# A bias table's load moved to the front of the DMA queue, one PSUM clear and two routing steps moved beside the first maxima

## The chip, the cores and the metric

The kernel runs on one core of a Trainium2 chip. The metric is the device time of one execution in microseconds (us), over several executions; a profile of one execution gives the time of each instruction on the engines: TensorE (PE, its weight loads PEld), VectorE (DVE), ScalarE (ACT), GpSimd (POOL), SyncE (SP), and of the DMA engines that SyncE's queue feeds.

## What is computed

Two residual layers over x of 16 sequences of 256 tokens with 128 features. Each layer adds attention times silu of a mixture of experts. The change lies in the first layer alone, at the start of its attention, whose reference is (cut):

```python
    def _L0_attn_ref(x, Wq, bq, Wk, bk, Wv, bv, Wo, bo, rel_bias):
        N_HEADS = 16
        ...
        Q, K, V = (proj(Wq, bq), proj(Wk, bk), proj(Wv, bv))
        scores = jnp.einsum('bhqd,bhkd->bhqk', Q, K) / math.sqrt(D_K)
        scores = scores + _rel_bias_matrix(rel_bias, S)[None]
        attn = jax.nn.softmax(scores, axis=-1)
        out = jnp.einsum('bhqk,bhkd->bhqd', attn, V)
        ...
    def _L0_ffn_ref(x, W1, b1, W2, b2, gate_W, shared_W, shared_b, gamma, beta):
        ...
        probs = jax.nn.softmax(flat @ gate_W, axis=-1)
        topk_w, topk_idx = jax.lax.top_k(probs, TOP_K)
```

`_rel_bias_matrix` gives each head a table of 256 x 256 that depends on the distance of two tokens alone. The routing needs, for each token, its eight gate logits less their maximum, their exponentials, and the two largest.

## The kernel before

All engines run hand-written programs, ordered by semaphores alone; nothing is scheduled by a compiler. The work is in stages, and `b` counts the 16 sequences.

**Setup.** SyncE queues, on one queue, x, the weights, and two small DRAM strips made from the relative bias (`extb_dram` in bf16, `ext_dram` in fp32). From them two tables are loaded, 128 rows x 16 heads x 384: `biasA` (bf16, 1536 KB) for the maxima, `biasT` (fp32, 3072 KB) for the scores proper. `biasA` is loaded at once. `biasT` is loaded only after the next stage.

**Projection** (`pre_pe`, `pre_act`, `pre_dve`), 16 turns. PE multiplies (L680 for queries and keys into banks 6 and 7, L687 for values, gate logits and the shared expert). ACT copies queries and keys out (L1059, L1060), then rounds them to bf16, the "hi" piece (L1066); DVE takes values and logits (L1355, L1356), and splits off two more pieces (L1345, L1347, L1349). SyncE stores the three pieces to `stk_dram` in three DMAs per turn, 768 KB (L377), and loads the stacks of the first two sequences among them (L388, L389). The pieces have a ring of three, so L1066 of turn b waits until the stores of turn b - 3 have landed. `keep_shared` (L1070) copies the shared expert's part, one turn later than L1066 of the same turn.

**First maxima** (sequence 0), eight pairs of heads t. PE computes scores with bias in wide[0] and wide[1] in turn (`max_scores`: L719 bias, L725 scores), DVE reduces them (`reduce_maxima`, L1541). PE's first one waits for the semaphore `init` at 3, and for all of L1070. After `max_scores` of t = 5 PE transposes the first four pairs' maxima (L738), ACT copies them out (L1113, `copy_maxima`), SyncE places them in the stacks by DMA (L395, `place_maxima`, which also waits for all stores of pieces). Only then can PE make the first exact scores (`exp_scores`, L750).

**Attention**, sequence by sequence. In each turn t of sequence b PE makes the scores of b (L750) and the maxima's scores of b + 1 (L719, L725). Every other pair's scores are biased by DVE (`add_bias`, L1550), the others are copied by ACT (`take_scores`, L1129) and biased by POOL (L599); both read `biasT`. ACT takes the exponential (L1136). The steps of the first routing stand between DVE's turns of sequences 0 to 3 (L1388 to L1507).

**Between** projection and maxima stand three small things: `route_shift(0)` (L1381, L1382: maximum of the logits, and the difference), its exponential on ACT (`route_act`, L1094), and the clear of bank 6 (L1532), which adds the last count of `init`. Bank 6 is the target of queries and keys of the even turns, and later that of the attention's outputs.

Of the kernel before, what the change touches and what calls it, by code (L numbers as in the profile page):

```python
# [5 lines left out]
NB, S, D = 16, 256, 128  # L6
P = 128
T = NB * S // P
H0, DK = 16, 8
MAXREL = 128  # L10
NREL = 2 * MAXREL + 1
E0, E1, HID = 8, 4, 512
# [35 lines left out]
EXT = 2 * S - 1  # L48
# [12 lines left out]
BW = S + P  # L61
# [67 lines left out]
def build(nc, x, wpack, vectors, shb, relb, wcat0, wcat1, out):  # L129
# [10 lines left out]
    with ctx:  # L140
# [197 lines left out]
        def _(sp):  # L338
# [4 lines left out]
            for dst, src in ((packed[:, 0:3 * D], wpack[:, 0:3 * D]),  # L343
# [11 lines left out]
            sp.dma_start(biasA[:, :, :], bass.AP(tensor=extb_dram.tensor, offset=0, ap=[[1, P], [EXT, H0], [1, BW]])  # L355
                         ).then_inc(s_ba, 16)

            emptied = [0, 0]
# [43 lines left out]
            for b in range(NB // 2, NB):  # L402
# [4 lines left out]
                if first < 4:  # L407
                    load_stacks(first // 2, first // 2, first % 2)
            sp.dma_start(biasT[:, :, :], bass.AP(tensor=ext_dram.tensor, offset=0, ap=[[1, P], [EXT, H0], [1, BW]])
                         ).then_inc(s_bt, 16)  # L410
            for u in range(NRING):
# [621 lines left out]
        def _(act):  # L1033
# [14 lines left out]
            def pre_act():  # L1048
# [7 lines left out]
                def projected(b, u, turn):  # L1056
# [4 lines left out]
                    if b >= NRING:  # L1061
                        act.wait_ge(m[f"stored{b % NRING}"], b // NRING * STORES * 16)
                    act.wait_ge(m["qkf"], b + 3)
                    if b == 2:
                        act.wait_ge(s_extd, 32)
# [6 lines left out]

                staged([(transposed, 1), (projected, 2), (keep_shared, 3)])

# [21 lines left out]
            pre_act()  # L1096
            route_act(0, E0)

# [70 lines left out]
            fetch_values(0, 0)  # L1169
            copy_maxima(0, 0)  # L1170
            attend_act(0, 0, back=0)
            attend_act(1, 1, back=1)
# [105 lines left out]
        def _(dve):  # L1278
# [56 lines left out]
            def pre_dve(l, ne):  # L1335
# [15 lines left out]
                def logits(b, u, turn):  # L1351
                    dve.wait_ge(m["gs"], b + 3)
                    dst = some(lg, b * 2, 2)[:, :, 0:ne]
                    vg = wide[1 + u][:, :].rearrange("p (j c) -> p j c", j=2)
                    V.tensor_copy(dst, vg[:, :, D:D + E0]).then_inc(m["lg"], 1)  # L1355
                    V.tensor_copy(some(vall, b * 2, 2), vg[:, :, 0:D]).then_inc(m["v"], 1)  # L1356

                staged([(logits, 3), (split, 3)])
# [170 lines left out]
            dve.wait_ge(s_c, 11)  # L1529
            route_shift(0)  # L1530
            dve.wait_ge(pre[0]["qkf"], NB + 2)
            V.memset(bank[6][:, :], 0.0).then_inc(A0["init"], 1)  # L1532

# [67 lines left out]
            for t in range(NPAIR):  # L1601
                reduce_maxima(0, t)
            dve.wait_ge(s_bt, 16)
            attend_dve(0, back=0, part=0)
# [306 lines left out]
```

## Time and profile before

| | us |
|---|---|
| median of 3 runs | 900.63 |
| lowest, highest | 898.08, 901.89 |
| profiled execution, its own time | 896.93 |
| its span in the trace | 894.6 |
| PE busy | 732.0 (82%) |
| DVE busy | 570.2 (64%) |
| ACT busy | 494.3 (55%) |
| POOL busy | 450.1 (50%) |

The trace's times count from the start of the span; 2.3 us lie around it. PE is the busiest engine over the whole, but the change acts between 14 us and 90 us, and there other waits end last: they are read from the rows below. A timeline row tells when a group of instructions began, how long it lasted, and in square brackets how long its engine had been idle and what ended the idle time.

### The profile page before, as it was taken

What the parts mean: (1) busy time and instruction counts of PE and PEld (TensorE: products, weight loads), DVE (VectorE), ACT (ScalarE), POOL (GpSimd) and SP (SyncE); (2) the same over time, 40 slices, a digit from 0 to 9 for tenths busy, and PEclk for the clock granted to TensorE, in tenths of its full rate; (3) what the DMA queues carried; (4) which work ended last, traced back from release to release, by engine and by line L of the source; (5) the groups of instructions that cost most, each with busy time, mean ns of one, the idle gap of its engine ahead of it and who ended that gap; (6) DMA issues with size and microseconds to landing.
All of it is one profiled execution on the core that took longest, in us unless ns stands there. A gap on an engine that the chain in (4) does not pass through costs nothing.

```text
span 894.6 us, 17583 instructions
## 1 busy us (share of the span) xinstructions
PE 732.0 (82%) x5530; PEld 501.5 (56%) x5530; DVE 570.2 (64%) x1284; ACT 494.3 (55%) x949; POOL 450.1 (50%) x394
## 2 busy tenths in 40 slices
PE   0966597879999999988799998899947775999940
PEld 0741132233343334336799988789847664999940
DVE  7867989878888888842243357845547881344445
ACT  0752475558887888774355546579631352555521
POOL 7901454458888988851355544410006671555540
PEclk9997788789999999968999999999977796999985
DMA  7697440112322232124777896550001115787837
GB/s 212 228 284 265 155 156 19 49 57 70 99 77 77 79 94 84 57 79 125 232 233 225 235 300 203 176 159 1 2 0 46 46 55 150 230 230 230 231 115 186
DMA packets 112239, 124.08 MB, mean 139 GB/s; under 512 B 10544, under 2 KB 93152, under 8 KB 112192
## 3 DMA queue, kind: packets, MB, share of 16 engines
q1 hardware_dynamic: 104064, 106.71, 40.2%
q0 software_dynamic: 8128, 16.78, 5.3%
q8 instruction: 25, 0.41, 0.2%
q14 instruction: 22, 0.18, 0.1%
HBM read 82.50 MB, written 40.81 MB: 138 GB/s over the span
## 4 chain that ended last, share of the span: by engine, by line
PE 58%; DVE 19%; DMA 6%; issue 6%; ACT 5%; SPq 4%; POOL 1%; ACTq 0%; DVEq 0%; POOLq 0%
PE wide L855 15%; PE wide L844 14%; PE wide L765 6%; PE wide L719 4%; PE wide L750 4%; PE wide L777 3%; ACT work L1129 2%; PE wide L725 2%; DVE work L1550 2%; DMA work<-xg_dram 2%; DVE work L1541 2%; PE wide L929 2%; ACT work L1136 2%; PE wide L938 1%; DMA biasT<-ext_dram 1%
## 5 line engine op out<-in xcount | busy, mean ns | idle before, releaser
L635 POOL DMA_INDIRECT yg_dram<-work x138 | 134.3, 973 | 171.3 <-DVE work L1648 148.8
L1192 ACT ACTIVATE work<-wide,work 128x256 f32<-128x256 f32 x324 | 131.9, 472 | 112.4 <-PE wide L844 111.3
L1541 DVE TENSOR_REDUCE work<-wide 128x4 bf16<-128x1024 f32 x128 | 156.5, 1226 | 38.8 <-PE wide L725 37.0
L855 PE MATMUL wide<-work 128*128 128x128 f32 x1296 | 158.8, 276 | 0.0
L855 PEld LDWEIGHTS wide<-work 128*128 128x128 f32 x1296 | 153.2, 193 | 0.6
L844 PE MATMUL wide<-xT,work 128*128 128x256 f32 x552 | 134.9, 388 | 9.7 <-issue 6.2
L844 PEld LDWEIGHTS wide<-xT,work 128*128 128x128 f32 x552 | 101.7, 194 | 23.9 <-issue 8.1
L599 POOL TENSOR_TENSOR work<-work,biasT 128x1024 f32<-128x1024 f32 x32 | 75.8, 2368 | 75.6 <-ACT work L1129 75.0
L599 POOL TENSOR_TENSOR yy<-yy,biasT 128x1024 f32<-128x1024 f32 x32 | 75.7, 2366 | 42.6 <-ACT yy L1129 42.5
L719 PE MATMUL wide<-biasA,turnb 128*128 128x512 bf16 x256 | 83.8, 412 | 5.8 <-DVE wide L1532 5.0
L1136 ACT ACTIVATE yy<-yy 128x1024 f32<-128x1024 f32 x64 | 67.5, 1057 | 38.0 <-DVE yy L1550 38.0
L1620 DVE COPY xT<-wide 128x256 f32<-128x256 f32 x69 | 29.2, 423 | 92.8 <-PE wide L866 81.3
L750 PE MATMUL wide<-work 49*128 49x256 bf16 x512 | 54.5, 295 | 32.6 <-DVE yy L1550 18.0
L1136 ACT ACTIVATE work<-work 128x1024 f32<-128x1024 f32 x64 | 67.3, 1052 | 16.0 <-DVE work L1550 16.0
L591 POOL DMA_INDIRECT xg_dram<-bufB,sloti x64 | 62.8, 981 | 13.5 <-issue 12.3
L750 PEld LDWEIGHTS wide<-work 49*128 49x128 bf16 x512 | 15.1, 96 | 81.0 <-issue 26.2
L1645 DVE TENSOR_TENSOR work<-wide,work 128x256 f32<-128x256 f32 x69 | 29.2, 423 | 45.5 <-PE wide L855 45.4
L591 POOL DMA_INDIRECT xg_dram<-bufC,sloti x52 | 50.2, 965 | 15.8 <-issue 13.7
L725 PE MATMUL wide<-work 48*128 48x256 bf16 x512 | 53.2, 289 | 0.0
L725 PEld LDWEIGHTS wide<-work 48*128 48x128 bf16 x512 | 14.9, 96 | 60.4 <-issue 60.4
L587 POOL TENSOR_SCALAR bufC<-tokf 128x32 f32<-128x32 f32 x2 | 0.7, 325 | 88.6 <-DVE widx L1507 86.6
L1129 ACT ACTIVATE yy<-wide 128x1024 f32<-128x1024 f32 x32 | 32.7, 1021 | 18.8 <-PE wide L750 18.8
(273 smaller groups left out, 1273.1 us busy)
## 6 DMA issues: line engine op xcount, KB each, us to landing
work<-in_wcat SPq DMA_DIRECT2D x73, 578.0 KB
work<-stk_dram SPq DMA_DIRECT2D x128, 96.0 KB, 2.5
xg_dram<-empty SPq DMA_DIRECT2D x35, 260.0 KB, 2.5
work<-xg_dram SPq DMA_DIRECT2D x69, 130.0 KB
yy<-yg_dram SPq DMA_DIRECT2D x14, 512.0 KB, 6.9
stk_dram<-yy SPq DMA_DIRECT2D x16, 384.0 KB, 3.0
stk_dram<-yy SPq DMA_DIRECT2D x16, 256.0 KB, 3.1
biasT<-ext_dram SPq DMA_DIRECT2D x1, 3072.0 KB, 12.4
```

The source lines that it names most:

```text
L591: g.indirect_dma_start(out=xg_dram[l], out_offset=bass.IndirectOffsetOnAxis(ap=sloti[k][:, t:t + 1].bitcast(u32), axis=0), in_=xn_sb[l][:, ...
L599: g.tensor_tensor(sc, sc, bass.AP(tensor=bt.tensor, offset=bt.offset + S - 1, ap=[list(bt.ap)[0], [BW, 2], [P, 2], [-1, S]]), ALU.add).the ...
L635: g.indirect_dma_start(out=yg_dram[l], out_offset=bass.IndirectOffsetOnAxis(ap=yid[v][:, s_:s_ + 1].bitcast(u32), axis=0), in_=yb[u][:, s_ ...
L719: mm(PA[t % 2][:, e * 2 * S:(e + 1) * 2 * S], turnb[:, :], bass.AP(tensor=b_.tensor, offset=b_.offset, ap=[list(b_.ap)[0], [P, 2], [1, S]] ...
L725: last = mm(PA[t % 2][:, (2 * e + c) * S:(2 * e + c + 1) * S], qst[u][pair_rows(e, TROWS), t, qt * P:(qt + 1) * P], kst[u][pair_rows(e, TR ...
L750: last = mm(PB[:, (2 * e + k) * S:(2 * e + k + 1) * S], kst[u][pair_rows(e), t, k * P:(k + 1) * P], qst[u][pair_rows(e), t, :], start=True ...
L765: last = mm(PO[32 * i:32 * i + DK + 1, 0:S], vaug[u][:, k, 4 * gr + i, :], sc[:, at:at + S], start=(k == 0), stop=(k == 1))
L844: last = mm(HP[u][c // 2][:, (c % 2) * TS:(c % 2 + 1) * TS], wb[v][:, c * P:(c + 1) * P], rows, start=True, stop=True)
L855: last = mm(YP[u][:, s_ * D:(s_ + 1) * D], hb[u][:, c, s_ * P:(s_ + 1) * P], wb[v][:, HID + c * D:HID + (c + 1) * D], start=(c == 0), stop ...
L1136: A(scores[t], scores[t], ACT.Exp).then_inc(a["E"], 1)
L1192: A(hb[u][:, c, :], bank[2 + 2 * u + c // 2][:, (c % 2) * TS:(c % 2 + 1) * TS], ACT.Gelu, bias=wb[v][:, bc:bc + 1]).then_inc(m["gelu"], 1)
L1541: V.tensor_reduce(nmax[:, :, 2 * t:2 * t + 2].rearrange("p c e -> p e c"), wide[t % 2][:, :].rearrange("p (e c k) -> p e c k", e=2, c=2), ...
```

## The change

Three edits.

1. The load of `biasT` is issued right behind that of `biasA`, ahead of all stores of pieces, and no longer behind the last of them.
2. The clear of bank 6 stands in DVE's stage `logits` of the last turn, ahead of the last split, and waits there for queries and keys of that turn. So that PE's wait for L1070 is met early too, ACT makes the last two `keep_shared` ahead of the last L1066; the first of the two stands behind the wait for the ring's stores.
3. `route_shift(0)` stands behind the fifth reduction of the first maxima (t = 4), and its exponential behind ACT's first copy of maxima.

```diff
@@ -354,6 +354,8 @@
             sp.dma_start(biasA[:, :, :], bass.AP(tensor=extb_dram.tensor, offset=0, ap=[[1, P], [EXT, H0], [1, BW]])
                          ).then_inc(s_ba, 16)
+            sp.dma_start(biasT[:, :, :], bass.AP(tensor=ext_dram.tensor, offset=0, ap=[[1, P], [EXT, H0], [1, BW]])
+                         ).then_inc(s_bt, 16)
@@ -406,8 +408,6 @@
                     load_stacks(first // 2, first // 2, first % 2)
-            sp.dma_start(biasT[:, :, :], bass.AP(tensor=ext_dram.tensor, offset=0, ap=[[1, P], [EXT, H0], [1, BW]])
-                         ).then_inc(s_bt, 16)
@@ -1061,6 +1061,9 @@
                     act.wait_ge(m["qkf"], b + 3)
+                    if b == NB - 1:
+                        keep_shared(b - 1, 1 - u, 0)
+                        keep_shared(b, u, 0)
@@ -1070,7 +1073,11 @@
-                staged([(transposed, 1), (projected, 2), (keep_shared, 3)])
+                def shared(b, u, turn):
+                    if b < NB - 2:
+                        keep_shared(b, u, turn)
+
+                staged([(transposed, 1), (projected, 2), (shared, 3)])
@@ -1094,7 +1101,6 @@
             pre_act()
-            route_act(0, E0)
@@ -1168,6 +1174,7 @@
             copy_maxima(0, 0)
+            route_act(0, E0)
             attend_act(0, 0, back=0)
@@ -1354,6 +1361,9 @@
                     V.tensor_copy(some(vall, b * 2, 2), vg[:, :, 0:D]).then_inc(m["v"], 1)
+                    if b == NB - 1:
+                        dve.wait_ge(m["qkf"], NB + 2)
+                        V.memset(bank[6][:, :], 0.0).then_inc(A0["init"], 1)
@@ -1527,9 +1537,6 @@
             dve.wait_ge(s_c, 11)
-            route_shift(0)
-            dve.wait_ge(pre[0]["qkf"], NB + 2)
-            V.memset(bank[6][:, :], 0.0).then_inc(A0["init"], 1)
@@ -1600,6 +1607,8 @@
                 reduce_maxima(0, t)
+                if t == 4:
+                    route_shift(0)
```

PE's own order is not touched. On ACT, the last turns of the projection and the first of the attention stand before as follows (pre0_v counts DVE's L1356, pre0_stored0 the landed stores of every third turn, route0_lgx is the end of L1382):

```order
L1059 ACTIVATE work<-wide3,more 128x256 [waits pre0_split,pre0_qkv]
L1060 ACTIVATE work<-wide3,packed 128x256
L1066 ACTIVATE yy<-work 128x2x256 [waits pre0_qkf,pre0_stored0]
L1070 ACTIVATE bufC<-wide1 128x2x128 [waits pre0_v]
L1070 ACTIVATE bufC<-wide2 128x2x128 [waits pre0_v]
L1094 ACTIVATE rt0<-rt0 128x256 [waits route0_lgx]
L1107 ACTIVATE work<-yy 128x32x8 [waits pre0_v,attend0_init,constants_made]
L1113 ACTIVATE work<-wide3 8x256 [waits attend0_mT]
```

and after the change (line numbers shift by 3 and more; L1073 is the old L1070, L1069 the old L1066, L1101 the old L1094):

```order
L1059 ACTIVATE work<-wide3,more 128x256 [waits pre0_split,pre0_qkv]
L1060 ACTIVATE work<-wide3,packed 128x256
L1073 ACTIVATE bufC<-wide1 128x2x128 [waits pre0_v,pre0_qkf,pre0_stored0]
L1073 ACTIVATE bufC<-wide2 128x2x128 [waits pre0_v]
L1069 ACTIVATE yy<-work 128x2x256
L1113 ACTIVATE work<-yy 128x32x8 [waits pre0_v,attend0_init,constants_made]
L1119 ACTIVATE work<-wide3 8x256 [waits attend0_mT]
L1101 ACTIVATE rt0<-rt0 128x256 [waits route0_lgx]
```

Both copies now stand ahead of the last rounding, and the wait for the ring's stores has gone with them. On DVE, from the last turn's logits to the sixth reduction of maxima (wide3 holds banks 6 and 7), before:

```order
L1355 COPY lg<-wide2 128x16 [waits pre0_gs]
L1356 COPY yy<-wide2 128x256
L1345 TENSOR_TENSOR work<-work,yy 128x512 [waits pre0_pieces,pre0_hi]
L1347 CAST yy<-work 128x2x256 [waits pre0_split]
L1349 TENSOR_TENSOR yy<-work,yy 128x512 [waits pre0_split]
L1381 TENSOR_REDUCE tmpa<-lg 128x32 [waits pre0_lg,constants_made]
L1382 TENSOR_TENSOR rt0<-lg,tmpa 128x256 [waits dve_steps]
L1532 MEMSET wide3 128x512 [waits pre0_qkf]
L1541 TENSOR_REDUCE work<-wide0 128x2x2 [waits attend0_A]
```

and after:

```order
L1363 COPY yy<-wide2 128x256
L1366 MEMSET wide3 128x512 [waits pre0_qkf]
L1352 TENSOR_TENSOR work<-work,yy 128x512 [waits pre0_pieces,pre0_hi]
L1354 CAST yy<-work 128x2x256 [waits pre0_split]
L1356 TENSOR_TENSOR yy<-work,yy 128x512 [waits pre0_split]
L1548 TENSOR_REDUCE work<-wide0 128x2x2 [waits attend0_A,constants_made]
L1548 TENSOR_REDUCE work<-wide1 128x2x2 [waits attend0_A]
L1548 TENSOR_REDUCE work<-wide0 128x2x2 [waits attend0_A]
L1548 TENSOR_REDUCE work<-wide1 128x2x2 [waits attend0_A]
L1548 TENSOR_REDUCE work<-wide0 128x2x2 [waits attend0_A]
L1391 TENSOR_REDUCE tmpa<-lg 128x32 [waits pre0_lg]
L1392 TENSOR_TENSOR rt0<-lg,tmpa 128x256 [waits dve_steps]
```

The clear has moved ahead of the last split, and the two routing steps from between split and reductions to behind the fifth reduction.

## Rows read from the trace of the kernel before

**Rows 1.** The chain of waits, 60 to 92 us: start, length, what.
```profile
68.91 0.64 ACT yy L1066
69.57 0.70 DVE work L1345
...
73.54 12.39 DMA biasT<-ext_dram
...
86.14 1.23 DVE work L1541
```

**Rows 2.** The timeline of DVE, 68 to 89 us: start, length, instruction, idle before.
```profile
68.25 0.41 DVE L1356 COPY yy<-wide 128x256 f32<-128x256 f32 x1
...
70.75 0.69 DVE L1349 TENSOR_TENSOR yy<-work,yy 128x512 bf16<-128x512 f32 x1
71.36 0.41 DVE L1381 TENSOR_REDUCE tmpa<-lg 128x32 f32<-128x256 f32 x1
71.81 0.42 DVE L1382 TENSOR_TENSOR rt<-lg,tmpa 128x256 f32<-128x256 f32 x1
72.34 0.48 DVE L1532 MEMSET wide<- 128x512 f32 x1
74.67 1.23 DVE L1541 TENSOR_REDUCE work<-wide 128x4 bf16<-128x1024 f32 x1 [1.85 <-PE wide L725]
76.18 8.20 DVE L1541 TENSOR_REDUCE work<-wide 128x4 bf16<-128x1024 f32 x7 [0.28 <-PE wide L725]
```

**Rows 3.** The timeline of PE, 73 to 86 us.
```profile
73.08 1.01 PE L719 MATMUL wide<-biasA,turnb 128*128 128x512 bf16 x2 [4.95 <-DVE wide L1532]
...
79.84 0.60 PE L719 MATMUL wide<-biasA,turnb 128*128 128x512 bf16 x2
80.70 0.28 PE L738 MATMUL wide<-identb,work 128*8 128x128 bf16 x2
...
84.79 0.39 PE L750 MATMUL wide<-work 49*128 49x256 bf16 x4 [1.69 <-DMA work<-work]
...
85.66 0.39 PE L725 MATMUL wide<-work 48*128 48x256 bf16 x4
```

**Rows 4.** The timeline of ACT and of SyncE's queue, 69 to 90 us.
```profile
69.44 0.64 ACT L1070 ACTIVATE bufC<-wide 128x256 f32<-128x256 f32 x2
...
81.01 0.37 ACT L1113 ACTIVATE work<-wide 8x256 bf16<-8x256 bf16 x1 [7.68 <-PE wide L738]
81.47 7.91 SPq L395 DMA_DIRECT2D work<-work  x4
```

**Rows 5.** The timeline of SyncE's queue, 9 to 30 us.
```profile
28.57 1.52 SPq L377 DMA_DIRECT2D stk_dram<-yy  x3
```

**Rows 6.** Stretches: busy time by engine, granted PE clock, DMA share, GB/s.
```profile
20.40:29.40 9.00, 7.05 (x26) 5.58 (x27) 4.49 (x15) 4.76 (x12) 8.08 (x11) 1.00 0.01 2
29.40:41.00 11.60, 10.46 (x50) 7.68 (x48) 11.15 (x26) 9.19 (x25) 11.60 (x11) 1.00 1.00 335
...
75.60:84.00 8.40, 6.62 (x42) 1.54 (x42) 8.12 (x8) 0.37 (x1) 0.00 (x0) 0.92 1.02 365
```

**Rows 7.** Stretches of the same columns, while the PE clock is low.
```profile
70.00:73.40 3.40, 0.32 (x1) 0.14 (x2) 2.62 (x6) 0.92 (x3) 0.00 (x0) 0.50 1.04 344
73.40:76.90 3.50, 3.50 (x14) 0.52 (x12) 1.95 (x2) 0.00 (x0) 0.00 (x0) 0.51 1.00 309
```

**Rows 8.** DMA issues, 0 to 130 us: KB each, median us from issue to landing.
```profile
yy<-in_relb SPq DMA_DIRECT2D x1, 16.1 KB, 1.9
```

**Rows 9.** The timeline of DVE and POOL, 90 to 111 us.
```profile
90.38 0.43 DVE L1390 TENSOR_TENSOR rt<-rt,tmpb 128x256 f32<-128x256 f32 x1
90.58 2.44 POOL L599 TENSOR_TENSOR work<-work,biasT 128x1024 f32<-128x1024 f32 x1 [1.81 <-ACT work L1129]
...
97.94 2.27 DVE L1408 TENSOR_TENSOR rt<-rt,hot 128x256 f32<-128x256 f32 x1
...
110.09 0.42 DVE L1408 TENSOR_TENSOR rt<-rt,hot 128x256 f32<-128x256 f32 x1
```

## The prediction

> **What bounds the kernel here.** I read the chain of waits between 60 us and 92 us first, then the timelines of the engines that it names, then the DMA share by stretch. The chain says that the projection ends on DMA: ScalarE's last rounding (L1066) starts at 68.91 us, when the stores of the piece ring have landed, and DVE splits from 69.57 us [rows 1]. Then it names one transfer, biasT, from 73.54 us for 12.39 us, and goes on with DVE's reduction at 86.14 us [rows 1]. Read alone, that promises up to twelve microseconds. The timelines say otherwise. Between 73.54 us and 86.14 us the first maxima are made anyway: DVE reduces from 74.67 us, then seven times in 8.20 us, to 84.38 us [rows 2]. And the reduction at 86.14 us waits for PE just as long as for biasT: its matmuls (L725) begin at 85.66 us and take 0.39 us, so they end at 86.05 us [rows 3], while biasT landed at 73.54 + 12.39 = 85.93 us [rows 1]. PE in turn stood until 84.79 us for the DMA that places the maxima [rows 3]. So three things end within some 0.2 us of each other; a gain needs all three earlier, and the change does touch all three. The quantity to follow is the start of the first reduction of sequence 1, now 86.14 us.
>
> **biasT's load.** Where it stands now, it moves its 3072 KB from 75.6 us to 84.0 us, 8.4 us at 365 GB/s [rows 6]. Where it goes, it is queued behind biasA, whose data are through by 20.4 us, and the DMA engines then are idle until the first pieces: share 0.01 over 9.0 us, against 1.00 over the 11.6 us behind it [rows 6]. 8.4 us fit into 9.0 us, with 0.6 us to spare; the first store is issued at 28.57 us [rows 5] and its data move from 29.4 us. PE, ACT, DVE and POOL all work in that stretch, but none of them waits for the DMA. I cost the move at nothing; without that cover, each microsecond by which biasT ends later than 29.4 us is one by which a saturated stream of stores ends later, and L1066's waits with it. The bound is -0 to 0.2 us if the rate is a little lower than 365 GB/s; the worst case is a rival below. On SyncE's queue nothing waits behind the issue: its next instruction is the store at 28.57 us.
>
> **ScalarE's two copies.** Both L1070 now run ahead of the last L1066, and behind the ring's stores, since that wait stands on the first of them. Two of them take 0.64 us, one has begun 0.27 us before the next [rows 4], so L1066 starts 2 x 0.27 = 0.54 us later, at 69.45 us, and the last split with it: it ends at 71.44 + 0.54 = 71.98 us [rows 2]. That is the price of the change on the path. In return PE's wait for them ends at about 69.6 us.
>
> **DVE's clear.** It takes 0.48 us [rows 2]. In its new place DVE is idle from 68.25 + 0.41 = 68.66 us to 69.57 us [rows 1, 2], 0.91 us, so it is hidden, and it would be so if it took twice as long. It ends near 69.2 us, ahead of the copies. So PE begins its maxima at 69.6 us and not at 73.08 us [rows 3], and the first two pairs are ready when DVE has done its split: even with the PE clock at 0.50 of full speed as it is there [rows 7] a pair takes 74.67 - 73.08 = 1.59 us, two 3.2 us, ready by 72.8 us. The reductions begin at 72.0 us, 2.7 us earlier than at 74.67 us.
>
> **The routing steps.** route_shift took 71.36 us to 72.23 us, 0.87 us [rows 2]. It is paid again behind the fifth reduction. Its exponential follows ACT's copy of maxima, where ACT idles until PE's L750. Nobody is queued behind it: DVE needs it only at L1390.
>
> **The chain to 86.14 us, with PE at full clock from about the third pair.** One reduction costs 8.20 / 7 = 1.17 us. The fourth ends at 72.0 + 4 x 1.17 = 76.7 us, the fifth at 77.85 us, the sixth (behind 0.9 us of route_shift) at 79.9 us, the seventh at 81.1 us. PE makes pair 5 behind the fourth and then transposes: L719 of that pair began at 79.84 us and the transpose at 80.70 us, 0.86 us apart, and L738 takes 0.28 us [rows 3]; now the transpose starts at 77.6 us and ends at 77.9 us, 3.1 us earlier. ACT's copy starts at 77.95 us. From the copy at 81.01 us [rows 4] to PE at 84.79 us [rows 3] it was 3.78 us, with biasT's data ahead in the queue. The lower bound for this is a copy of 0.37 us, 0.09 us to the issue, one of the two DMAs issued 0.58 us behind the other (an estimate: four in 7.91 us with a long pause, a short one takes about as long as L377's third of 1.52 us, 0.5 us [rows 4, 5]), and 1.9 us to land as the smallest load did [rows 8]: 2.9 us. So L750 starts between 80.9 us and 81.75 us, 3.9 to 3.05 us earlier than 84.79 us. PE itself is free by then: pair 7 waits for the sixth reduction (79.9 us) and takes 0.9 us, 80.8 us. The next reduction follows L750 by 86.14 - 84.79 = 1.35 us: 82.3 to 83.1 us.
>
> **PE's clock.** The granted clock is 0.50, the lower level of 1.2 GHz, from 70.0 us, where PE worked 0.32 us of 3.40 us, up to nearly 76.9 us, through a stretch in which PE worked without a pause [rows 7]; from 75.6 us to 84.0 us its mean is 0.92 [rows 6]. Now PE works from 69.6 us to 72.8 us and on. If the rise comes with it, the working above holds. If it stays low until 76.9 us, pairs 2 and 3 cost 1.5 us and not 1.17 us each, pair 4 some more: the fourth reduction ends at 77.4 us, the sixth at 80.8 us, L750 starts at 82.0 us, and the gain is 2.8 us (2.1 us with the long placing). The Trainium skill, TensorE: Matmul & The Clock Gate, Part 1 (the clock gate), says that activity releases the throttle and that idleness restores it; by that rule alone the rise would come forward as far as PE's start does, and the gain would be the full 3.9 us. No row here shows a mostly busy stretch at the low clock with a gap in it, so I keep both.
>
> **The sum.** Gain 3.9 us at best and 2.1 us at worst on this path; I take 3.4 us, since the short placing is nearer to what an empty queue does, and the clock can be either. Less 0.1 us for biasT's fit: 3.3 us. What follows (POOL's and DVE's biases, the routing, the attention) hangs on this start and shifts as a whole; nothing there stands at a fixed time. Against the profiled execution's own time: 896.93 - 3.3 = 893.6 us, or 0.37% less. That execution is 3.7 us below the median of the runs, 900.63 us; the forecast is for the median: 900.63 - 3.3 = 897.3 us. Own range of this case: 896.7 to 898.5 us, from gains of 3.9 and 2.1 us. What a measurement can tell from no change is 0.5%, 4.5 us, which this forecast stays under.
>
> **Rivals.** *A hold turns against it.* L1390 starts at 90.38 us, 0.2 us ahead of POOL's addition at 90.58 us, and takes 0.43 us; L1408, started under an addition of POOL, took 2.27 us where it takes 0.42 us alone [rows 9]. If the routing step falls 0.2 us later against POOL, L1390 is held for about 2.2 us on DVE's path: gain 3.3 - 2.2 = 1.1 us, 899.5 us. Against it: both follow the same addition of DVE, so their distance should stay. The Trainium skill, SBUF — State Buffer, on the shared port pair, says that a DVE instruction with two SBUF inputs and a GpSimd one that reads SBUF lock each other out for a whole instruction; by that rule the trace agrees, at 2.27 us against 0.42 us. *A hold turns in its favour.* The same mechanism: 2.27 - 0.42 = 1.85 us are lost at 97.94 us, and the routing's other steps up to L1507 stand beside POOL's additions too; with one and a half such holds gone, or PE's clock low for less of the first sequences, the gain is some 6 us, 894.6 us. *Only biasT moves.* If PE's start is held by something else, or the placing waits for the last stores (which, 0.54 us later now, must land before 78.4 us), the gain is what lies between the three waits, 0 to 1 us: 900.1 us. *The slower side.* biasT's 8.4 us don't fit the gap, because the queue takes the two tables together more slowly or starts late; the stores then stand behind them, and the saturated stream (share 1.00 behind 29.4 us [rows 6]) ends later by as much. It turns the result from a delay of 3.3 us on; with all of it late the loss is 8.4 - 3.3 = 5.1 us, 905.7 us. Against it: 0.6 us to spare by two measured stretches.
>
> **How the numbers follow.** Forecast 0.5; hold against it 0.15; in its favour 0.2; only biasT 0.08; slower side 0.07. The range reaches from 893.6 us to 901.4 us: it leaves out gains over 7 us and most of the slower side, together under 0.2. Faster by over 0.5% (below 896.1 us) is the favourable case and a little of the forecast: 0.27. Slower by over 0.5% (above 905.1 us) is part of the last: 0.05. Within: 0.68.
>
> **What would show it.** PE's first L719 of the attention at 69.6 us; the last L1066 at 69.45 us; the DMA share near 1 from 20.4 us to 29 us and at most a few tenths between 77 us and 84 us; the first reduction at 72.0 us and one of sequence 1 at 82.3 to 83.3 us; L750 first at 80.9 to 82.0 us, released by the placing DMA or by PE's own order, never by biasT. L1066's first waits for a store should stand where they were. It is wrong if L1066 comes later than 69.8 us (the stream was delayed), if L750 still starts behind 83 us, or if the shift found at 83 us isn't found again behind L1507, where the routing is over.

## The result: the changed kernel, and its profile

The changed kernel takes 895.74 us (median of 20 executions, 887.49 to 900.18) against 900.5 us (20 executions, 890.7 to 904.86): ratio 0.9947, 95% interval 0.9927 to 0.9967. A second measurement on another occasion gave 895.6 us against 901.2 us, again 0.9947 (0.9925 to 0.9969). The profiled execution takes 895.56 us, its span is 893.1 us. The forecast was 897.3 us. The ratios here and below leave out three slow executions: one of the kernel with PE kept busy (2379 us), and two of the kernel before on the first chip of the experiments (932 and 934 us).

The chain of waits of the changed kernel between 60 us and 92 us (start, length, what; lines answer to [rows 1]):

```profile
66.04 3.08 DMA stk_dram<-yy
69.14 0.05 ACT bufC L1073
...
69.42 0.38 ACT bufC L1073
69.80 0.52 ACT yy L1069
70.34 0.70 DVE work L1352
...
72.14 1.24 DVE work L1548
...
81.87 0.32 PE wide L725 x4
82.19 0.39 PE wide L750 x4
...
83.55 1.23 DVE work L1548
```

biasT has gone from the chain. ScalarE's two copies (now L1073) stand ahead of the last rounding (L1069), as [rows 4] had them behind it. The first reduction of sequence 1 starts at 83.55 us, where it was 86.14 us. The stretches of the same kernel (columns as in [rows 6]: busy time of PE, PE's weight loads, DVE, ACT and POOL, granted PE clock, DMA share, GB/s), the first and the last answering to [rows 6], the middle two to [rows 7]:

```profile
20.40:29.40 9.00, 7.08 (x24) 5.66 (x24) 4.13 (x15) 4.12 (x10) 7.95 (x10) 1.00 0.94 332
...
70.00:73.40 3.40, 3.06 (x12) 0.53 (x12) 2.99 (x5) 0.62 (x2) 0.00 (x0) 0.50 0.98 325
73.40:76.90 3.50, 3.48 (x14) 0.66 (x14) 2.78 (x3) 0.00 (x0) 0.00 (x0) 0.50 0.61 204
...
75.60:84.00 8.40, 7.00 (x45) 1.64 (x44) 7.73 (x9) 1.81 (x3) 0.17 (x1) 0.84 0.01 3
```

The idle stretch ahead of the stores is filled (0.94, was 0.01), the one from 75.6 us on is empty (0.01, was 1.02). PE is busy from 70.26 us where it was idle, and its clock is low all the same, until 78.2 us (76.8 us in the second trace of this kernel). DVE's timeline, against [rows 2]:

```profile
67.54 0.41 DVE L1363 COPY yy<-wide 128x256 f32<-128x256 f32 x1
68.06 0.48 DVE L1366 MEMSET wide<- 128x512 f32 x1
70.34 0.69 DVE L1352 TENSOR_TENSOR work<-work,yy 128x512 f32<-128x512 f32 x1 [1.80 <-ACT yy L1069]
...
72.14 2.45 DVE L1548 TENSOR_REDUCE work<-wide 128x4 bf16<-128x1024 f32 x2
75.04 1.23 DVE L1548 TENSOR_REDUCE work<-wide 128x4 bf16<-128x1024 f32 x1 [0.45 <-PE wide L725]
76.55 1.23 DVE L1548 TENSOR_REDUCE work<-wide 128x4 bf16<-128x1024 f32 x1 [0.27 <-PE wide L725]
78.05 1.23 DVE L1548 TENSOR_REDUCE work<-wide 128x4 bf16<-128x1024 f32 x1 [0.28 <-PE wide L725]
79.19 0.41 DVE L1391 TENSOR_REDUCE tmpa<-lg 128x32 f32<-128x256 f32 x1
79.64 0.42 DVE L1392 TENSOR_TENSOR rt<-lg,tmpa 128x256 f32<-128x256 f32 x1
79.98 4.80 DVE L1548 TENSOR_REDUCE work<-wide 128x4 bf16<-128x1024 f32 x4
```

The clear lies in idle time. The third to fifth reduction each wait for PE, which at the low clock needs 1.50 us for a pair where DVE needs 1.17 us. The reduction of sequence 1 is held by PE too: in the chain above, PE's pair behind the sixth reduction (L725, 81.87 us) and L750 (82.19 us) follow each other without a pause.

### The profile page after: what moved, and what is told of

It is laid out like the page before. It is cut to its first block, busy times and chain, and to the rows that moved or that the text cites. A ratio compares the mean times of both kernels' runs of the same rounds, so it can differ in the third digit from the quotient of the medians.

```text
span 893.1 us, 17583 instructions
## 1 busy us (share of the span) xinstructions
PE 734.1 (82%) x5530; PEld 502.7 (56%) x5530; DVE 570.8 (64%) x1284; ACT 494.6 (55%) x949; POOL 450.5 (50%) x394
## 4 chain that ended last, share of the span: by engine, by line
PE 57%; DVE 20%; issue 7%; DMA 6%; ACT 5%; SPq 3%; POOL 1%; ACTq 0%; DVEq 0%; POOLq 0%
PE wide L844 13%; PE wide L855 13%; PE wide L765 5%; PE wide L719 5%; PE wide L750 4%; PE wide L777 3%; PE wide L725 3%; ACT work L1135 2%; DVE work L1557 2%; DVE work L1548 2%; DMA work<-xg_dram 2%; PE wide L929 2%; DMA yg_dram<-work 2%; ACT work L1142 2%; PE wide L938 1%
## 5 line engine op out<-in xcount | busy, mean ns | idle before, releaser
L844 PE MATMUL wide<-xT,work 128*128 128x256 f32 x552 | 135.5, 390 | 9.5 <-issue 6.3
L844 PEld LDWEIGHTS wide<-xT,work 128*128 128x128 f32 x552 | 102.2, 195 | 23.9 <-issue 8.6
L1142 ACT ACTIVATE yy<-yy 128x1024 f32<-128x1024 f32 x64 | 67.5, 1057 | 38.3 <-DVE yy L1557 38.3
L719 PE MATMUL wide<-biasA,turnb 128*128 128x512 bf16 x256 | 85.1, 417 | 4.3 <-ACT bufC L1073 3.1
L1629 DVE COPY xT<-wide 128x256 f32<-128x256 f32 x69 | 29.2, 423 | 89.9 <-PE wide L866 77.5
L750 PE MATMUL wide<-work 49*128 49x256 bf16 x512 | 54.0, 292 | 31.0 <-DVE yy L1557 17.6
L591 POOL DMA_INDIRECT xg_dram<-bufB,sloti x64 | 62.8, 981 | 13.4 <-issue 12.4
L750 PEld LDWEIGHTS wide<-work 49*128 49x128 bf16 x512 | 15.1, 96 | 79.5 <-issue 25.3
L725 PE MATMUL wide<-work 48*128 48x256 bf16 x512 | 53.7, 291 | 0.0
L725 PEld LDWEIGHTS wide<-work 48*128 48x128 bf16 x512 | 14.9, 96 | 61.6 <-issue 61.6
```

Source lines behind the costliest of these rows:

```text
L591: g.indirect_dma_start(out=xg_dram[l], out_offset=bass.IndirectOffsetOnAxis(ap=sloti[k][:, t:t + 1].bitcast(u32), axis=0), in_=xn_sb[l][:, ...
L719: mm(PA[t % 2][:, e * 2 * S:(e + 1) * 2 * S], turnb[:, :], bass.AP(tensor=b_.tensor, offset=b_.offset, ap=[list(b_.ap)[0], [P, 2], [1, S]] ...
L725: last = mm(PA[t % 2][:, (2 * e + c) * S:(2 * e + c + 1) * S], qst[u][pair_rows(e, TROWS), t, qt * P:(qt + 1) * P], kst[u][pair_rows(e, TR ...
L750: last = mm(PB[:, (2 * e + k) * S:(2 * e + k + 1) * S], kst[u][pair_rows(e), t, k * P:(k + 1) * P], qst[u][pair_rows(e), t, :], start=True ...
L844: last = mm(HP[u][c // 2][:, (c % 2) * TS:(c % 2 + 1) * TS], wb[v][:, c * P:(c + 1) * P], rows, start=True, stop=True)
L1142: A(scores[t], scores[t], ACT.Exp).then_inc(a["E"], 1)
```

## The experiments

My theory was: three ends come within a microsecond of each other (biasT's landing, the placing DMA, PE's own pace at the low clock), the change moves all of them, and the gain is what the maxima's earlier start leaves. The rivals: biasT alone is the gain; or its load isn't free; or the gain is another one than the traces' path shows.

The first four kernels ran on a chip on which the kernel before takes 925.25 us (35 executions); the others on chips where it takes 899.6 to 901.2 us. Ratios are against the kernel before on the same chip. They are those of the measurement and not the quotient of the two medians beside them, from which they differ by up to 0.002; their intervals reach 0.002 to 0.004 to either side. So the kernels below whose ratios lie within 0.003 of each other are put in order by their traces alone, one trace each. Places of the first 90 us are compared between traces of both kinds; the span differs by some 30 us between them, and how much of that lies in the first 90 us has no trace of before to tell, so differences under 1 us across chips are not leaned on.

**Only biasT's load moved.**

```diff
 (against the kernel before)
             sp.dma_start(biasA[:, :, :], ...).then_inc(s_ba, 16)
+            sp.dma_start(biasT[:, :, :], ...).then_inc(s_bt, 16)
...
-            sp.dma_start(biasT[:, :, :], ...).then_inc(s_bt, 16)
```

> The kernel before with the load of biasT behind that of biasA, and nothing else. My account (biasT, the placing DMA and PE's matmuls end within 0.2 us of each other, so removing one gives little): the first maxima start at 73.1 us as before, the copy of maxima at 81.0 us; with nothing ahead of it in the queue the placing needs at most the 2.96 us that it needed in the changed kernel, so the first L750 starts at 84.0 us and the first reduction of sequence 1 at 85.3 us: gain 0.8 us, 899.7 us. The chain of waits read alone (biasT is 12.4 us of it) would give a gain of several us. If the early load delayed the stores, the last L1066 would come later than 68.9 us.

Measured: 923.99 us against 925.25 us, ratio 0.9967 (0.9934 to 1.0, so it can be told neither from no change nor from the whole change's 0.9947). PE and DVE in its trace:

```profile
85.26 0.39 PE L750 MATMUL wide<-work 49*128 49x256 bf16 x4 [0.96 <-DMA work<-work]
```
```profile
75.56 1.23 DVE L1541 TENSOR_REDUCE work<-wide 128x4 bf16<-128x1024 f32 x1 [1.84 <-PE wide L725]
...
86.61 1.23 DVE L1541 TENSOR_REDUCE work<-wide 128x4 bf16<-128x1024 f32 x1 [1.03 <-PE wide L725]
```

The reduction of sequence 1 starts at 86.61 us, within the kernel before's 86.14 to 87.12 us (three traces, below). biasT no longer waits anywhere, and the wait has passed to PE, behind the placing DMA. What the placing gained (2.98 us from the copy at 82.28 us, against 3.78 us in [rows 3, 4]) was lost ahead of it: the last L1066 came at 69.80 us, 0.9 us later than in [rows 1]. The next kernel, on the same chip without the early load, had the ring's stores landed at 69.17 us, so some 0.6 us of that may be the early load's, and my expectation of 85.3 us was too early by 1.3 us. On this chip the load was issued at 14.79 us and took 15.1 us, to 29.9 us, where the changed kernel's took from 14.38 us to 29.4 us: the 0.6 us to spare were used up. The chain's 12.4 us of biasT were worth nothing on this path alone.

**All but biasT's load.** The same two lines of biasT as above, the other way round, in the changed kernel.

> The changed kernel with the load of biasT back behind the last store; clear, copies and routing steps stay moved. My account: biasT's data move from some 76 us to 84.5 us and land at 86.3 to 86.6 us, and DVE's first reduction of sequence 1 waits for that: gain 0 us or a loss of up to 0.5 us against before, although the first maxima begin 2.5 us earlier. Rival (the load was a mere neighbour on the chain, and the gain of 2.7 us comes from the maxima's earlier start): that reduction stays at 83.5 us and the gain is 2.7 us.

Measured: 927.19 us against 925.25 us, ratio 1.0001 (0.9968 to 1.0034). Its chain of waits:

```profile
73.83 13.40 DMA biasT<-ext_dram
87.23 0.02 issue
87.25 1.23 DVE work L1548
```

The maxima begin as early as in the changed kernel (first reduction at 72.17 us), and everything is lost to biasT, which lands at 87.23 us. So neither part moves the reduction of sequence 1 by itself, and both together do: the two are one change. The traces show this; the ratios alone would not.

**Routing steps back ahead of the maxima.**

```diff
 (against the changed kernel)
             dve.wait_ge(s_c, 11)
+            route_shift(0)
...
                 reduce_maxima(0, t)
-                if t == 4:
-                    route_shift(0)
```

In this kernel ACT's exponential stayed where the change has it.

> The changed kernel with route_shift and its exponential back ahead of the first maxima, the clear and biasT as changed. My account: the first reduction starts 0.87 us later, at 73.0 us; the fifth is the last one that is later, but the copy of maxima and the placing hang on the fourth, so the first L750 starts at about 83.1 us and the first reduction of sequence 1 at 84.4 us, 0.9 us behind the changed kernel: gain 1.8 us against before. Rival (the position of the two steps doesn't matter, since DVE has the same work ahead of sequence 1 either way): 83.5 us, gain 2.7 us.

Measured: 924.49 us against 925.25 us, ratio 0.9973 (0.9941 to 1.0005). The first reduction at 73.75 us, the copy of maxima at 80.62 us, L750 at 83.59 us (waiting 0.83 us for the placing), the reduction of sequence 1 at 84.94 us. Against the changed kernel's two traces (83.55 and 83.07 us) that is 1.4 to 1.9 us later, of which its last rounding at 70.50 us (69.68 and 69.43 us there) explains 0.8 to 1.1 us; some 0.6 to 0.8 us are left for the two steps, near the 0.9 us expected. The path through the placing is right; the amount is within the spread of two traces and compares two chips, so it isn't leaned on. The ring's stores landed at 69.96 us here, also on the first chip and with the early load, 0.8 us later than the 69.17 us without it.

**biasT inside the stream of stores.**

```diff
 (against the changed kernel)
-            sp.dma_start(biasT[:, :, :], ...).then_inc(s_bt, 16)
...
             for b in range(NB // 2):
                 store_pieces(b, b % NRING)
+                if b == 3:
+                    sp.dma_start(biasT[:, :, :], ...).then_inc(s_bt, 16)
```

> The changed kernel with the load of biasT behind the stores of the fourth turn, so inside the saturated stream and not in the idle stretch ahead of it. My account (its 8.4 us cost nothing only because the DMA engines were idle): the last L1066 comes 7 to 8.4 us later, at 76 to 77.5 us, the first reduction of sequence 1 at 90.5 to 92 us, and the kernel is 4.5 to 6 us slower than before, 905 to 906.5 us. Rival (the stores wait for landing times, not for bandwidth, and take the load in their gaps): the last L1066 within 2 us of 69.1 us, the gain mostly kept.

Measured: 928.56 us against 925.25 us, ratio 1.0043 (1.0013 to 1.0073). ScalarE in its trace (one more line number than the changed kernel's):

```profile
77.78 0.66 ACT L1074 ACTIVATE bufC<-wide 128x256 f32<-128x256 f32 x2 [2.33 <-DMA stk_dram<-yy]
78.33 0.63 ACT L1070 ACTIVATE yy<-work 128x512 bf16<-128x512 f32 x1
```

The ring's last stores landed at 77.78 us, 8.6 us later than 69.14 us (or than the 69.17 us of the kernel without the early load on this chip): the whole of biasT's 8.4 us. The reduction of sequence 1 came at 91.61 us. This prices the fourth rival of the prediction and shows that the load costs little only because of the idle stretch.

**Copies ahead of the wait for stores.**

```diff
 (against the changed kernel)
+                    if b == NB - 1:
+                        keep_shared(b - 1, 1 - u, 0)
+                        keep_shared(b, u, 0)
                     if b >= NRING:
                         act.wait_ge(m[f"stored{b % NRING}"], b // NRING * STORES * 16)
                     act.wait_ge(m["qkf"], b + 3)
-                    if b == NB - 1:
-                        keep_shared(b - 1, 1 - u, 0)
-                        keep_shared(b, u, 0)
```

> The changed kernel with ScalarE's last two keep_shared ahead of the wait for the ring's stores, not behind it. My account (the two copies cost 0.54 us on the path only because the wait stands on the first of them): the copies run at 66.7 us and 68.0 us, in ACT's idle time; the last L1066 starts at 69.1 us and not 69.7 us, PE's maxima at 68.6 us and not 70.3 us, the first reduction 0.54 us earlier, and PE's clock may rise one to two us earlier; the first reduction of sequence 1 at 82.2 to 83.0 us: gain 3.2 to 4.0 us against before. Rival (PE at the low clock sets the pace of the reductions, so DVE's earlier start is lost again): 83.5 us, gain 2.7 us.

Measured: 897.16 us against 899.59 us, ratio 0.9962 (0.9938 to 0.9986). The last rounding started at 68.83 us and PE at 68.79 us; the first reduction at 71.28 us, but the copy of maxima only at 78.55 us and the reduction of sequence 1 at 82.86 us. From 0.6 to 0.9 us of earlier start 0.2 to 0.7 us are left: PE at the low clock took the rest (the third to fifth reduction wait 0.54, 0.28 and 0.28 us for it). By its ratio this kernel gains no more than the changed one.

**And the routing steps in DVE's idle time.**

```diff
 (against the kernel with the copies first)
                         V.memset(bank[6][:, :], 0.0).then_inc(A0["init"], 1)
+                        dve.wait_ge(s_c, 11)
+                        route_shift(0)
...
                 reduce_maxima(0, t)
-                if t == 4:
-                    route_shift(0)
```

> As copies_first, and route_shift right behind the clear, in DVE's idle time before its last split, not between the fifth and sixth reduction. My account: 0.87 us fit into the idle time of 1.8 us that the changed kernel's trace shows there, as long as the copies are out of the way: the gap is then 1.2 us, so they just fit; the sixth reduction comes 0.87 us earlier, the first reduction of sequence 1 at 81.7 to 82.5 us, limited by the placing of the maxima (copy plus 2.9 us): gain 3.6 to 4.6 us against before. Rival (the placing DMA sets the pace): as copies_first.

Measured: 896.03 us against 899.59 us, ratio 0.9972 (0.9946 to 0.9999). The steps fit the gap, the last rounding stayed at 69.04 us, but the reduction of sequence 1 came at 82.90 us, as in the kernel before this one: L750 at 81.55 us is 2.97 us behind the copy. The rival held.

**PE kept busy.**

```diff
 (against the changed kernel)
-            for name in ("xT", "qkf", "v", "lg", "sh"):
+            pe.wait_ge(pre[0]["xT"], NB + 2)
+            pe.wait_ge(pre[0]["qkf"], NB + 2)
+            for _ in range(5):
+                mm(bank[7][:, 0:2 * P], ident[:, :], xT[1][:, :], start=True, stop=True)
+            for name in ("v", "lg", "sh"):
                 pe.wait_ge(pre[0][name], NB + 2)
```

> The changed kernel with five matmuls that nobody reads in PE's idle time between its last projection and the first maxima (67.2 to 70.3 us in the changed kernel's trace), written to bank 7; output unchanged. My account (the low clock costs about 1.1 us there: 2.8 us of gain instead of 3.9): PE stays at the full clock through the maxima, pair 2 to 4 cost DVE's 1.17 us each, and the first reduction of sequence 1 comes at 82.4 us and not 83.5 us: gain 3.8 us. Rival (the clock had fallen for an idle stretch earlier, at 62 us to 66 us, and the five matmuls run slowly): maxima start late, at 71 us or more, gain under 2.7 us.

Measured: 894.88 us against 899.59 us, ratio 0.9947 (0.9925 to 0.9968). PE and DVE in its trace (L703 are the five matmuls, two records each):

```profile
67.52 3.27 PE L703 MATMUL wide<-xT,ident 128*128 128x256 f32 x10
70.62 0.59 PE L723 MATMUL wide<-biasA,turnb 128*128 128x512 bf16 x2
71.15 0.39 PE L729 MATMUL wide<-work 48*128 48x256 bf16 x4
```
```profile
71.65 5.83 DVE L1552 TENSOR_REDUCE work<-wide 128x4 bf16<-128x1024 f32 x5
...
81.83 1.23 DVE L1552 TENSOR_REDUCE work<-wide 128x4 bf16<-128x1024 f32 x1 [0.17 <-PE wide L729]
```

The clock came back at 69.4 us, the five reductions take 5.83 us, DVE's own 1.17 us each and no wait for PE. The reduction of sequence 1 starts at 81.83 us, 1.2 to 1.7 us before the changed kernel's. Its last rounding happened to start 0.3 to 0.5 us earlier as well (69.14 us), so 0.9 to 1.2 us are what the low clock costs on this path. In this trace the clock had fallen earlier than in the changed kernel's first trace, at 62.6 us and not at 68.0 us: that half of my rival came true, but the maxima did not start late for it. The ratio, 0.9947, is the changed kernel's own, so the microsecond is seen in the trace alone.

**The same eight times in the kernel before.** Eight such matmuls there, and nothing of the change.

> The kernel before with eight unread matmuls in PE's idle time between its last projection and the first maxima, and nothing of the change. It measures what the low clock costs there by itself. The maxima then run at the full clock: pair 0 ready 0.5 us earlier, reductions from 74.2 us in 1.17 us each, copy of maxima at 80.1 to 80.5 us; but biasT lands at 85.9 us as before and its wait holds the first reduction of sequence 1 at 86.1 us: gain 0 to 0.3 us. Rival (the clock is worth a microsecond whatever else waits): gain 1 us or more.

Measured: 897.14 us against 901.2 us, ratio 0.9975 (0.9956 to 0.9993). The times of my account held, its reasons only in part. The copy of maxima came at 80.52 us, and the reduction of sequence 1 at 86.59 us, inside the kernel before's own spread. But the clock did not stay high: only the first pair ran at it wholly, then it was at 0.50 from 74.1 to 77.5 us and again from 84.4 us on. And what held the reduction of sequence 1 was PE at this low clock, though the profile names biasT. That transfer had landed at 85.68 us, while PE's matmuls ended at 86.49 us:

```profile
84.38 0.61 PE L754 MATMUL wide<-work 49*128 49x256 bf16 x4 [1.84 <-DMA work<-work]
84.91 1.04 PE L723 MATMUL wide<-biasA,turnb 128*128 128x512 bf16 x2
85.88 0.61 PE L729 MATMUL wide<-work 48*128 48x256 bf16 x4
```

The attention ends no earlier either (the eight matmuls of L844, here L848, stand at 409.64 us, and at 408.27, 408.68 and 409.16 us in the three traces of before). Yet the median is 4.1 us lower, by the ratio 2.3 us. By this run alone a gain can be measured that no place of a trace shows.

**All three.** Copies first, routing steps in the gap, four unread matmuls.

> The changed kernel with the two copies ahead of the wait for stores, route_shift right behind the clear, and four unread matmuls in PE's idle time, all at once. By the sum of the single traces: DVE's first reduction at 71.2 to 71.7 us, the full clock from some 69.5 us, no routing steps among the reductions; the copy of maxima at 76.8 us, the first L750 2.97 us behind it at 79.8 us (the placing DMA sets the pace), the first reduction of sequence 1 at 81.2 us: gain 5 us against before, 0.7 us better than the unread matmuls alone. Rival (the last sequences of steps are bound by the placing in any case): as the unread matmuls alone, 81.8 us, gain 4.3 us.

Measured: 893.71 us against 901.2 us (8 executions), ratio 0.9935 (0.9908 to 0.9961), the lowest of all, though its interval overlaps the changed kernel's. Its trace:

```profile
80.27 0.39 PE L754 MATMUL wide<-work 49*128 49x256 bf16 x4 [0.88 <-DMA work<-work]
```
```profile
71.45 9.22 DVE L1554 TENSOR_REDUCE work<-wide 128x4 bf16<-128x1024 f32 x8
81.63 1.23 DVE L1554 TENSOR_REDUCE work<-wide 128x4 bf16<-128x1024 f32 x1 [0.95 <-PE wide L729]
```

DVE is now through with its eight reductions at 80.7 us and idles 0.95 us; PE waits 0.88 us for the placing. The copy at 77.30 us plus 2.97 us sets the pace, and with the routing steps among the reductions it was 81.83 us: 0.2 us of difference, the rival's side. The lead isn't even kept in this trace: the matmuls of L844 near the end of the attention (here L848) stand at 404.97 us, in the changed kernel's traces at 405.84 and 404.87 us, with the clock low for 48 us between 90 us and 210 us here and for 39 and 44 us there.

**The changed kernel again, and the kernel before twice more.**

> The changed kernel, unchanged. Its traces gave 2.6 to 3.2 us at the first reduction of sequence 1 (83.55 us against 86.14 and 86.73 us), its medians 4.8 us. Account A (the surplus of some 2 us is chance of the granted clock: in 20 executions of the changed kernel the mean clock was 0.9124, in 35 of the kernel before 0.9084, and 0.01 of mean clock goes with 4 to 5 us in both): now the gain is 2 to 4 us, ratio 0.996 to 0.998, and the mean clock within 0.002 of before's. Account B (an earlier start of PE's work raises the granted clock in every execution): again 0.9947, and the mean clock 0.004 higher.

> The kernel before, unchanged, for a second trace of it. In the first trace the lead of the changed kernel was 2.7 us from 90 us to 400 us and shrank to 1.5 us at the end; by my account this shrinking is PE's clock falling at other places in the expert loops from run to run. Then a second trace of the kernel before differs from the first by some 1 to 4 us in the expert loops, and by under 0.5 us up to 85 us.

> The kernel before, unchanged, for a third trace. Its two profiled executions took 896.9 and 898.4 us, both under the median of 60 unprofiled ones (900 us), and a kernel that shifts nothing on the path (eight unread matmuls, reduction of sequence 1 at 86.6 us) still measured 3 to 4 us under it. Account A (typical executions of the kernel before lose some 2 to 4 us to the low clock at a place that the first two traces didn't catch, in the attention's first sequences or the expert loops): a third execution near 900 us shows more time at the low clock, by 8 to 15 us, and the place of it. Account B: it is again near 897 us, and where the surplus comes from stays open.

Measured: 0.9947 for the changed kernel as said above; 1.0006 (0.9979 to 1.0033) and 1.0 (0.997 to 1.0031) for the kernel before against itself. Where the traces stand, in us:

| trace | L750 | reduction of sequence 1 | end of span |
|---|---|---|---|
| before, three traces | 84.79, 85.38, 84.90 | 86.14, 86.73, 87.12 | 894.6, 896.0, 895.6 |
| changed, two traces | 82.19, 81.72 | 83.55, 83.07 | 893.1, 891.4 |

The means are 86.66 us and 83.31 us: 3.35 us. For L750 they are 85.02 us and 81.96 us: 3.07 us. The difference is the clock: in the third trace of before it fell at 84.6 us, and PE's matmuls behind L750 (L719, L725) took 1.04 and 0.61 us there, where the first trace has 0.61 and 0.39 us. In the second and third traces of before DVE's wait ahead of this reduction ends with PE and not with biasT, the one that [rows 1] names; this bears out that the ends lie together. Behind the routing the lead is still there: its last step, L1507 (L1517 in the changed kernel), stands at 185.2, 185.6 and 186.1 us in the traces of before and at 182.3 and 183.1 us in those of the changed kernel, 2.9 us apart in the mean. At the end of the span the means are 895.4 us and 892.25 us: 3.15 us.

The rest of the measured gain goes with the granted clock. Over all executions with a clock on record on the chips of the 900 us kind, 85 of the kernel before took 900.14 us in the mean at a mean clock of 0.9084, and 32 of the changed kernel 895.59 us at 0.9115. Within each kernel a slower execution has a lower clock; one line fitted to both with a step between them gives 4.0 us for 0.01 of clock (standard error 0.6), and a step of 3.3 us (standard error 0.5). So of 4.55 us, 1.2 us go with the clock, and 3.3 us are left, about what the path shows. This is a correlation, and the step is no measure of the path: the same fit gives the kernel before with eight unread matmuls a step of 1.6 us (standard error 0.6), though its reduction of sequence 1 came no earlier, and a step of 3.9 us (0.7) to the changed kernel with PE kept busy, whose reduction came 4.8 us earlier.

Of the two accounts of the second measurement neither held whole. The mean clock was 0.9100 against 0.9080, within the 0.002 of account A (chance), but the gain of 4.8 us was above its 2 to 4 us; account B had the gain right and half of its 0.004 of clock. Whether the change raises the clock stays open. The third trace of the kernel before, too, is of an execution under its usual time (897.96 us), so at which place its usual executions lose the rest is open.

## Why the prediction was nearly right, step by step

**What bounds it.** Right. Three waits end together, and taking one away passes the wait on: only biasT gave a reduction at 86.61 us, all but biasT 87.25 us, the two together 83.1 to 83.6 us. Reading the chain alone, with 12.4 us of biasT on it, would have misled.

**biasT free of charge.** Right within 0.2 us in the changed kernel: the ring's stores landed at 69.14 us, where L1066 had started at 68.91 us. In the second trace they landed at 68.89 us. On the first chip of the experiments it was not free: the stores landed 0.6 and 0.8 us later in the two traces with the load in its new place (69.80 and 69.96 us) than in the one without (69.17 us). The margin of 0.6 us was thinner than it looked.

**The two copies, 0.54 us.** Right: 69.14 us to 69.68 us. **The clear, hidden.** Right: it starts at 68.06 us, and DVE is idle for 1.80 us more behind it.

**PE's start.** 69.6 us expected, 70.26 us found (70.01 us in the second trace). The second copy ends at 69.80 us and PE starts 0.46 us behind that; I had allowed 0.05 us. It cost nothing, for the reductions wait for the split: 72.14 and 71.89 us, 72.0 us expected.

**PE's clock.** Both branches were named, and the worse one came, in the first trace worse than named: the clock returned at 78.2 us, not at 76.9 us (76.8 us in the second). The fourth reduction ended at 77.78 us (77.4 us expected), L750 started at 82.19 us (82.0 us expected), the gain on the path between the first two traces was 2.6 us (2.8 us expected for this branch). By the rule of the Trainium skill, TensorE: Matmul & The Clock Gate, Part 1, the rise should have come forward with PE's work; the trace doesn't agree as I had used it: PE worked 3.06 us of 3.40 us from 70.0 us on at 0.50, and stayed at 0.50 through the next stretch. The prediction also misread the start. It let the low clock begin at 70.0 us, with PE's idle time, but in the trace that it used the clock was low from 63.2 us on, while PE was busy for 2.16 us of 3.40 us:

```profile
63.20:66.60 3.40, 2.16 (x7) 1.21 (x5) 1.72 (x5) 1.62 (x4) 0.00 (x0) 0.50 0.93 261
66.60:70.00 3.40, 1.53 (x4) 0.67 (x2) 1.82 (x5) 1.10 (x4) 0.00 (x0) 0.50 1.05 359
```

The three traces of the kernel before have it low from 63.2 to 76.9, from 67.0 to 77.3 and from 67.5 to 77.8 us, the two of the changed kernel from 68.0 to 78.2 and from 63.2 to 76.8 us. So PE's earlier start by 3 us did not bring the return forward, and one kernel differs from trace to trace by some 4 us in the fall. With unread matmuls ahead of the maxima and no idle time behind them the clock was back at 69.4 and 70.0 us (two traces); with eight of them and 2.56 us of idle time behind, it fell at 74.1 us.

**The placing.** The lower bound of 2.9 us was the right one: 2.96 to 2.98 us from the start of the copy of maxima to L750 in all nine traces without biasT in the queue (in the changed kernel's first trace PE's own matmuls end at the same moment, and the chain names them), against 3.63 to 4.17 us in the three traces of before and 5.67 us in the kernel with all but biasT.

**The sum.** 3.3 us forecast for the path; 3.35 us by the means of the traces at the reduction of sequence 1, 3.07 us at L750, 3.3 us at equal clock by the fit. That the figure is met so closely is in part luck. It was a middle value between two branches for the clock, and the worse branch came: from the 86.14 us that the prediction started from, the gain is 2.6 and 3.1 us in the two traces, near its 2.8 us. The other two traces of before stand 0.6 and 1.0 us later than that 86.14 us and make up the rest. The step that did not hold is the last one: that the clock is the same in both kernels. The changed kernel's executions have 0.003 more of mean clock, which goes with 1.2 us, and the median lies at 895.74 us, 1.6 us under the forecast and under its own range of 896.7 us, though within the whole range. That also put the result just past 0.5%, the side to which I had given 0.27.

**The rivals.** The holds did not turn where it was looked at: L1400, the old L1390 of [rows 9], starts at 87.78 us and POOL's addition at 87.98 us, again 0.2 us apart, and the held step took 2.27 us again:

```profile
87.78 0.42 DVE L1400 TENSOR_TENSOR rt<-rt,tmpb 128x256 f32<-128x256 f32 x1
...
95.36 2.27 DVE L1418 TENSOR_TENSOR rt<-rt,hot 128x256 f32<-128x256 f32 x1
```
```profile
87.98 2.44 POOL L599 TENSOR_TENSOR work<-work,biasT 128x1024 f32<-128x1024 f32 x1 [1.81 <-ACT work L1135]
```

With a lead of 2.9 us at L1507 in the mean, no hold of the first routing was gained or lost to speak of. The slower side is real and priced (8.6 us at the ring's stores), but the idle stretch was wide enough, save for the 0.6 to 0.8 us on the first chip. That only biasT moves did not happen: PE started at 70.26 us, and the placing took 2.96 us. The run of biasT alone shows what it would have been worth: the reduction of sequence 1 at 86.61 us, no gain.

## What to carry to other kernels

A transfer that fills the chain of waits is worth what the second latest wait leaves, not its own length: before moving it, look up when each other thing that the waiting instruction needs is ready, and move those together. A load that can be issued early belongs in a stretch where the DMA share is near zero, with a margin: 0.6 us to spare was enough on one chip and not on another. Inside a saturated stream the same load cost its whole 8.4 us, and behind the stream it delayed the small transfer queued after it. And small gains should be checked against the granted clock over many executions and several traces of each kernel: here a quarter of the measured gain went with the clock and could be given no place in the traces, and a kernel that moved nothing on the path still measured 2.3 us faster.

## What the hardware showed

- PE's granted clock stayed at 0.50 for 8 us of nearly continuous work (70.3 us to 78.2 us, two stretches of 3.06 of 3.40 us and 3.48 of 3.50 us) after an idle time of 3.1 us. With unread matmuls in that idle time it was low from 62.6 us and back at 69.4 us, PE having worked on from 65.6 us. In three traces of one unchanged kernel it fell at 63.2, 67.0 and 67.5 us.
- Executions with a lower mean clock take longer: 4.0 us for each 0.01 (standard error 0.6). That accounts for a fifth of the variance among the 85 executions of the kernel before (894.6 to 905.4 us) and for two fifths among the 32 of the changed one (887.5 to 900.2 us).
- Two DMAs of 2 KB each took 2.96 to 2.98 us from the start of the copy that fed them to the matmul that needed them, in nine traces on chips of both speeds, and up to 5.67 us behind 3 MB in the same queue.
- VectorE's L1408 (L1418 in the changed kernel), started under an addition of GpSimd, took 2.27 us in both kernels, and 0.42 us without one (in the kernel before).
